# Slot logits of a soft mixture-of-experts layer: computed twice in two layouts, or once, stored and transposed

## The reference, cut to what matters

```
logits = (einsum('tzd,ed->tze', x, phi_w) + phi_b).reshape(t, z, n, p)
D = softmax(logits, axis=3)          # over the 32 slots of an expert
C = softmax(logits, axis=2)          # over the 64 experts of a slot
X_tilde = einsum('tznp,tzd->npd', D, x)      # summed over all 8 entries
X_tilde = tanh(normalise(clip(X_tilde)))
Y_tilde = einsum('npd,ndH->npH', X_tilde, expert_w) + expert_b
Y = einsum('tznp,npH->tzH', C, Y_tilde)
```

## Time and profile before

| what | value |
|---|---|
| median of 3 runs | 1195.12 us (1194.73 to 1200.56) |
| the profiled execution's own time | 1194.49 us |
| its span, first to last instruction | 1192.6 us |
| busy: PE, PEld, DVE, ACT, POOL | 1032.1, 765.7, 765.5, 518.0, 158.1 us |
| mean granted clock of PE | 0.948 |
| HBM read, written | 33.16 MB, 1.06 MB |
| mean DMA rate | 29 GB/s |

### The profile page before, as it was taken

One profiled execution on the slowest core, in us unless ns is written; L12 is line 12 of the kernel. 1 busy time (PEld: TensorE's weight loads), 2 busy tenths in 40 slices (PEclk: granted clock), 3 DMA queues, 4 the chain that ended last, 5 costly groups with the idle time before them and its releaser, 6 DMA issues.

```text
span 1192.6 us, 18208 instructions
## 1 busy us (share of the span) xinstructions
PE 1032.1 (87%) x6734; PEld 765.7 (64%) x6760; DVE 765.5 (64%) x1829; ACT 518.0 (43%) x836; POOL 158.1 (13%) x166
## 2 busy tenths in 40 slices
PE   3989999998648899999999953788999999998755
PEld 2878888886436667776766733566666666666432
DVE  4565555554574678888888777536567676676432
ACT  1245445435322554465557312235455536543510
POOL 1120110100307300000000004201212022011000
PEclk9999999999768999999999987999999999999976
DMA  8010000000300221001300003000000000000000
GB/s 319 2 28 15 14 15 14 14 14 2 124 0 1 85 93 54 17 38 53 124 1 1 1 1 107 1 1 1 1 6 1 6 1 5 6 1 6 5 5 5
DMA packets 11800, 35.39 MB, mean 30 GB/s; under 512 B 2570, under 2 KB 5818, under 8 KB 10944
## 3 DMA queue, kind: packets, MB, share of 16 engines
q1 hardware_dynamic: 10464, 33.14, 7.8%
q10 hardware_dynamic: 1152, 1.05, 0.3%
q0 software_dynamic: 96, 0.04, 0.0%
HBM read 33.16 MB, written 1.06 MB: 29 GB/s over the span
## 4 chain that ended last, share of the span: by engine, by line
PE 58%; issue 18%; DVE 15%; DVEq 4%; ACT 2%; POOL 1%; POOLq 1%; another core or an unknown queue 0%; ACTq 0%
PE ps L1118 5%; PE ps L1104 5%; PE ps L836 5%; PE ps L1001 3%; PE ps L1046 3%; PE ps L1258 3%; PE ps L1179 3%; PE ps L1159 2%; DVE arena L1822 2%; PE ps L1197 2%; PE ps L870 2%; PE ps L1021 2%; PE ps L846 2%; PE ps L882 2%; PE ps L994 2%
## 5 line engine op out<-in xcount | busy, mean ns | idle before, releaser
L1926 DVE TENSOR_REDUCE arena<-ps 128x8 f32<-128x2048 f32 x32 | 73.3, 2291 | 37.3 <-PE ps L1159 37.3
L1465 ACT ACTIVATE arena<-ps 128x2048 f32<-128x2048 f32 x32 | 60.1, 1879 | 57.5 <-PE ps L1183 57.5
L1104 PE MATMUL ps<-uR,arena 128*128 128x256 f32 x256 | 74.6, 386 | 0.1
L1258 PE MATMUL ps<-arena 128*128 128x512 f32 x128 | 68.2, 657 | 5.5 <-DVE xacc L2000 4.4
L1021 PE MATMUL ps<-arena,uR 128*128 128x512 f32 x128 | 67.7, 610 | 3.5 <-ACT arena L1411 3.0
L1046 PE MATMUL ps<-arena 128*128 128x128 f32 x512 | 64.9, 281 | 6.7 <-DVE arena L1838 5.0
L1046 PEld LDWEIGHTS ps<-arena 128*128 128x128 f32 x512 | 62.4, 196 | 12.1 <-issue 7.9
L1118 PE MATMUL ps<-arena 128*128 128x256 f32 x256 | 63.9, 395 | 6.6 <-DVE arena L1907 3.7
L1438 ACT ACTIVATE arena<-ps 128x512 f32<-128x512 f32 x64 | 38.0, 598 | 60.5 <-PE ps L1105 54.1
L1118 PEld LDWEIGHTS ps<-arena 128*128 128x128 f32 x256 | 47.9, 194 | 20.0 <-issue 9.6
L836 PE MATMUL ps<-arena 128*128 128x256 f32 x256 | 58.0, 384 | 0.0
(11 more groups left out here) (381 smaller groups left out, 2355.5 us busy)
## 6 DMA issues: line engine op xcount, KB each, us to landing
arena<-in_skills SPq DMA_DIRECT2D x16, 768.0 KB, 5.7
arena<-in_expert_w SPq DMA_DIRECT2D x2, 2048.0 KB, 8.3
arena<-in_l_experts SPq DMA_DIRECT2D x8, 386.5 KB, 3.1
arena<-in_consts_b SPq DMA_DIRECT2D x1, 1152.0 KB, 9.5
x2R<-in_x ACTq DMA_DIRECT2D x8, 128.0 KB, 6.5
arena<-in_L_w SPq DMA_DIRECT2D x2, 512.0 KB, 12.1
arena<-in_phiC SPq DMA_DIRECT2D x1, 1024.0 KB, 12.6
arena<-in_expert_b SPq DMA_DIRECT2D x1, 1024.0 KB, 4.9
```

Source lines behind the costliest of these rows:

```text
L1104: mm(o, phiC[:, st_ * P:(st_ + 1) * P], uR[:, b, :], start=True, stop=False)
L1258: last = mm(low[:, 3, :], pm[:, 2 + j, k * P:(k + 1) * P], w2e[:, j, c * 512:(c + 1) * 512], start=j == 0, stop=j == 1)
L1465: av(pexp[:, t, gp].rearrange("p c h t -> p (c h t)"), scores[:, :, :].rearrange("p c t -> p (c t)"), ACT.Exp, scale=SCALE3).then_inc(s.sc ...
L1926: V.tensor_reduce(nm[:, k, :, 2 * gp:2 * gp + 2], scores[:, :, :].rearrange("p c (h t) -> p c h t", h=2), X, ALU.max, negate=True).then_in ...
```

## The change

The logits are made once, in LG. ACT's new step LC copies each tile out of PSUM into `raw` (four buffers of 1024 words, in the place of the no longer needed `hid`), DVE's LG takes both maxima there for 1024 slots at once, POOL's new step DS adds the negated maximum over slots and writes `eD`, and ACT's SH takes the exponential in SBUF. SP's new step KP stores each `raw` in a DRAM scratch. MT, SH and MC of PE and the copies of MT and MC of ACT are gone. LG of PE has three PSUM banks in place of two.

For the softmax over experts SP's new step BACK reads the logits of an entry back, tokens in partitions; POOL's CM adds the negated maximum over experts, ACT's CE takes the exponential, POOL's CA adds the halves, DVE's CB sums the rest, REC inverts, PE's CR transposes the reciprocals and DVE's RC copies them; PE's TC transposes the exponentials, and DVE's CN multiplies out of PSUM into `eC`, of which there is now one. CL, CSA, CSB and CSUM are gone. EWA and EWB load later, since `expert_w` goes where `hid` and `raw` lie. The constants `samep`, `selD`, `selP` go, and with them POOL's PX and some memsets. All of ORDER_BD is new. One wait for ACT's own pipe (a drain) is put ahead of SQ2. The core of the diff, by engine:

```diff
     # SP
-    LOAD.0 LOAD.1 LOAD.2 EWA.0 LOAD.3 LOAD.4 LOAD.5 LOAD.6 EWB.0 LOAD.7 EBD.0 ST.0 ST.1 ST.2 ST.3 ST.4 ST.5 ST.6
+    KP0.3 KP1.3 KP2.3 KP3.3 LOAD.6 KP0.4 KP1.4 KP2.4 KP3.4 LOAD.7 KP0.5 KP1.5 KP2.5 KP3.5 EWA.0 KP0.6 KP1.6 KP2.6
+    KP3.6 BACK.0 KP0.7 KP1.7 KP2.7 KP3.7 EWB.0 BACK.1 EBD.0 BACK.2 BACK.3 BACK.4 BACK.5 ST.0 BACK.6 ST.1 BACK.7 ST.2
...
+                for j in range(4):
+                    if n == f"KP{j}":
+                        sp.wait_ge(s.raw_copied, at(b, 8, 2 * j + 1))
+                        sp.dma_start(raw_d[b, j // 2, j % 2], raw[j]).then_inc(kept[j], 16)
+                if n == "EWB":
+                    sp.wait_ge(s.max_ready, 8 * NB)
+                    sp.wait_ge(s.shifted, 4 * NB)
+                    for j in range(4):
+                        sp.wait_ge(kept[j], 16 * NB)
...
+                if n == "BACK":
+                    if b == 0:
+                        sp.wait_ge(s.uC_mm, NB)
...
+                    for k in range(K):
+                        sp.dma_start(cT[u][k].rearrange("p (h c) -> p h c", h=2),
+                                     raw_d[b, :, k].rearrange("h p c -> p h c")).then_inc(raw_back[u], 16)
     # PE
-                        mm(high[:, c, :], uR[:, b, k * P:(k + 1) * P], phiC[:, col:col + 512], start=True, stop=False)
-                        mm(high[:, c, :], ones_rows, phib3[:, col:col + 512], start=False, stop=True).then_inc(s.lg_mm, 1)
+                        bank = high[:, LG_BANK[i % 3], :]
+                        mm(bank, uR[:, b, k * P:(k + 1) * P], phiC[:, col:col + 512], start=True, stop=False)
+                        mm(bank, ones_rows, phib3[:, col:col + 512], start=False, stop=True).then_inc(s.lg_mm, 1)
...
-                        mm(o, phiC[:, st_ * P:(st_ + 1) * P], uR[:, b, :], start=True, stop=False)
-                        last = mm(o, selPx[:, st_, :], mcR[:, b, :], start=False, stop=True)
+                        for k in range(K):
+                            st_ = 2 * a + t
+                            last = tr(low[:, a % 2, t * T + k * P:t * T + (k + 1) * P], cT[u][k][:, st_ * P:(st_ + 1) * P], ident)
     # ACT
+                    if n == f"LC{st_}":
+                        act.wait_ge(s.lg_mm, at(b, 8, st_))
...
+                        av(raw[j][:, c * 512:(c + 1) * 512], high[:, LG_BANK[i % 3], :], ACT.Copy).then_inc(s.raw_copied, 1)
+                    if n == f"SH{j}":
+                        act.wait_ge(s.shifted, at(b, 4, j))
+                        av(eD[j // 2][:, j % 2, :], eD[j // 2][:, j % 2, :], ACT.Exp).then_inc(s.eD_ready, 1)
+                    if n == f"CE{k}":
+                        act.wait_ge(s.c_shifted, at(b, 2, k))
+                        av(cT[u][k], cT[u][k], ACT.Exp).then_inc(s.c_exp, 1)
     # DVE
+                        lg = raw[j].rearrange("p (n q) -> p n q", q=PSLOT)
+                        V.tensor_reduce(nmd[j % 2], lg, X, ALU.max, negate=True).then_inc(s.max_ready, 1)
+                        V.tensor_reduce(nmc[:, k, h, :], lg.rearrange("p n q -> p q n"), X, ALU.max,
+                                        negate=True).then_inc(s.max_ready, 1)
+                        V.reduce_sum(csum[:, k * PSLOT:(k + 1) * PSLOT], halved[k].rearrange("p (n q) -> p q n", q=PSLOT),
+                                     X).then_inc(s.csum_ready, 1)
-                    some = eC[u][:, 4 * q:4 * q + 4, :]
-                    V.tensor_tensor(some, some, rC.unsqueeze(1).to_broadcast([P, 4, T]), ALU.mult).then_inc(s.C_ready, 1)
+                    V.tensor_tensor(eC[:, 2 * a:2 * a + 2, :], low[:, a % 2, :].rearrange("p (t c) -> p t c", t=2),
+                                    rC.unsqueeze(1).to_broadcast([P, 2, T]), ALU.mult).then_inc(s.eC_ready, 1)
     # POOL
-    W.0 WA.0 W.1 RSZ.0 WA.1 W.2 WA.2 W.3 RSZ.1 WA.3 W.4 WA.4 W.5 WA.5 RSZ.2 W.6 WA.6 W.7 WA.7 RSZ.3 RSZ.4 RSZ.5
+    W.0 W.1 WA.1 W.2 WA.2 W.3 WA.3 W.4 WA.4 W.5 WA.5 W.6 WA.6 W.7 WA.7 RSZ.0 RSZ.1 DS0.0 DS1.0 RSZ.2 DS2.0 RSZ.3 DS3.0
...
+    RSZ.7 DS0.5 DS1.5 DS2.5 DS3.5 DS0.6 DS1.6 DS2.6 DS3.6 CM0.0 CM1.0 DS0.7 DS1.7 CA0.0 DS2.7 CA1.0 DS3.7 CM0.1 CM1.1
+    JR0.0 VZ.0 JR1.0 CA0.1 CA1.1 CM0.2 CM1.2 CA0.2 QM.0 CA1.2 CM0.3 CM1.3 CA0.3 CA1.3 QM.1 CM0.4 CM1.4 RS1.0 CA0.4
...
+                        tile = [P, 32, PSLOT]
+                        G.tensor_tensor(eD[h][:, k, :].rearrange("p (n q) -> p n q", q=PSLOT),
+                                        raw[j].rearrange("p (n q) -> p n q", q=PSLOT),
+                                        nmd[j % 2].unsqueeze(2).to_broadcast(tile), ALU.add).then_inc(s.shifted, 1)
+                        G.tensor_tensor(c, c, mcA[:, b, k * PSLOT:(k + 1) * PSLOT].unsqueeze(1).to_broadcast([P, NSLOT, PSLOT]),
+                                        ALU.add).then_inc(s.c_shifted, 1)
+                        G.tensor_tensor(halved[k], cT[u][k][:, 0:HALF], cT[u][k][:, HALF:2 * HALF], ALU.add).then_inc(s.c_halved, 1)
```

More of the change, by code:

```diff
@@ L162 @@
[L162 to L166, removed]
@@ L249 @@
[L249 to L253 removed]
+    BC0.0 BC1.0 Z.0 ZT.0 BC0.1 SG0.0 SU0.0 SG1.0 SU1.0 SG2.0 SU2.0 SG3.0 SU3.0 SG4.0 SU4.0 SG5.0 SU5.0 BC1.1 UC.0 Z.1
@@ new lines @@
+    DS0.1 DS1.1 DS2.1 DS3.1 RSZ.4 DS0.2 DS1.2 DS2.2 DS3.2 DS0.3 RSZ.5 DS1.3 DS2.3 DS3.3 DS0.4 RSZ.6 DS1.4 DS2.4 DS3.4
+    RSZ.7 DS0.5 DS1.5 DS2.5 DS3.5 DS0.6 DS1.6 DS2.6 DS3.6 CM0.0 CM1.0 DS0.7 DS1.7 CA0.0 DS2.7 CA1.0 DS3.7 CM0.1 CM1.1
+    JR0.0 VZ.0 JR1.0 CA0.1 CA1.1 CM0.2 CM1.2 CA0.2 QM.0 CA1.2 CM0.3 CM1.3 CA0.3 CA1.3 QM.1 CM0.4 CM1.4 RS1.0 CA0.4
+    CA1.4 QM.2 CM0.5 CM1.5 CA0.5 CA1.5 RS1.1 RS2.0 QM.3 CM0.6 CM1.6 CA0.6 CA1.6 RS1.2 QM.4 RS2.1 CM0.7 CM1.7 CA0.7
+    RS1.3 CA1.7 QM.5 RS2.2 RS1.4 RS2.3 QM.6 RS1.5 QM.7 RS2.4 RS1.6 RS2.5 RS1.7 RS2.6 RS2.7""",
@@ L608, in build @@
         pexp = flat.rearrange("p (k a b h t) -> p k a b h t", k=K, a=2, b=4, h=2)
-        eC = [te([P, ST, T]) for _ in range(2)]
+        eC = te([P, ST, T])
+        cT0 = te([P, K, 2 * HALF])
         xn = te([P, ST, P])
@@ L1105, in step_d @@
-                        last = mm(o, selPx[:, st_, :], mcR[:, b, :], start=False, stop=True)
-                    last.then_inc(s.cl_mm, 1)
-                if n == "CSUM":
-                    pe.wait_ge(s.csum_ready, at(b))
-                    if b == 0:
-                        pe.wait_ge(s.b_loaded, all_b)
-                    mm(low[:, 0, 0:T], con("samep"), csumS[:, :], start=True, stop=True).then_inc(s.csum_mm, 1)
+                        for k in range(K):
+                            st_ = 2 * a + t
+                            last = tr(low[:, a % 2, t * T + k * P:t * T + (k + 1) * P], cT[u][k][:, st_ * P:(st_ + 1) * P], ident)
@@ L1117, in step_d @@
                     for t in range(4 * q, 4 * q + 4):
-                        last = mm(low[:, 1, 0:T], ytl[:, t, :], eC[u][:, t, :], start=t == 0, stop=t == ST - 1)
+                        last = mm(low[:, 1, 0:T], ytl[:, t, :], eC[:, t, :], start=t == 0, stop=t == ST - 1)
                     if q == 3:
@@ L1492, in step_d @@
                 if n == "SQ2":
+                    act.drain()
                     act.wait_ge(s.y3_ready, at(b))
```

444 lines of the change are left out of this document (198 added, 246 removed).

## The result

The changed kernel takes 1229.83 us (median of 4 runs, 1228.26 to 1232.32) against 1197.05 for the kernel before on the same chip: ratio 1.0273, interval 1.0238 to 1.0308. It is **slower**, where the prediction said 1166. The profiled execution has a span of 1230.5 us, 37.9 more than before.

The account below looks back on a forecast made before the run. PE was taken to set the pace, with DVE close behind in B. The terms 7 - 13 + 2 - 25 = -29 on 1194.5 gave 1166 us; the forecast's own bounds were 1150 to 1190, the wider range 1135 to 1200.

Parts of the forecast that it names:

- The start, +7: Start of B: POOL's back-to-back sums and products hold five DVE operations, first BC 7 us later; bounds 0 and 10.
- B, -13: Steady B: PE drops 2.3 us a batch, about 0.4 given back to POOL holding DVE; 1.9 x 7 = 13 us earlier.
- Tail and join, +2: From UC.7's end to Y0.0: BACK, CM, DS, CA and EWB queues take 81 us against 79, 2 us later.
- D, -25: Steady D: TC cheaper than CL saves PE 5.4 us a batch, a third given back; 3.6 x 7 = 25 us earlier.
- I let a third of POOL's time reach DVE: Steady D: POOL's 16 us a batch adds 5 to DVE's 35, giving 40, under PE's 42.
- a third of the 5.4: Steady D: the part of PE's 5.4 us saving a batch given back because PE will wait at times, leaving 3.6.
- PE stays fed: Rival: POOL and DVE seldom meet; B gives 29, D 38, start costs nothing, join 2: 1130 us; chance 0.2.
- GpSimd holds VectorE: Rival: every DS, CM, CA and QM stops DVE for its whole length, in B and D: 1245 us; chance 0.14.
- Late reads: Rival: 2 MB reads take 15 us, JR0.0 slips, join costs 17 instead of 2: 1181 us; chance 0.1.
- TC no cheaper: Rival: TC costs as much as CL because its four weight loads show; D gives nothing: 1190 us; chance 0.06.

Follow-up runs that it names:

- the five other runs with this start: The changed kernel with short CM, short reads, neighbouring words, only D's steps, or fourteen moves: 1183.05, 1194.65, 1214.85, 1168.92, 1191.28 us.
- the run with the old products' order: The changed kernel with only the first 23 steps of POOL's list reordered, RSZ.0 again behind two products W: 1229.34 us.
- the new lists: The changed kernel, same steps, with the order in PE, ACT, DVE and POOL lists of B and D laid out from its own trace: 1122.66 us.
- fitting lists: The changed kernel with lists laid out from measured durations, once (1122.66 us) and once more from the durations of that run (1113.21 us).
- shorter reads: The changed kernel with its own lists, BACK of entries 2 to 7 reading 128 of each 1024 words: 1194.65 us.
- below 1184: The kernel before with lists found in the same way from its own trace, as long a search: 1184.16 us.
- the short CM: CM on 64 words in place of 2048: 1183.05 us with the changed kernel's own lists; with new lists and neighbouring-word reduces as well, 1102.05 us.
- the lists at 1123 and 1113 us: The changed kernel with lists laid out from its own trace (1122.66 us), then once more from the durations of that run (1113.21 us).

## Why the prediction was wrong, point by point

**The start, +7.** The first BC came 7.7 us later (4.4 to 6.7 in the five other runs with this start), and the run with the old products' order shows the reason to be the one given. The size was in part luck: the prediction had five operations of DVE held, three near 331 us and two near 351. In the trace seven took 1.98 to 2.41 us between 324 and 340 us, where two did before, and none near 351. The step from there to the end was wrong: only 1.7 us were left at UC.0.

**B, -13; it was +19.6.** The work was about right: UC.0 to UC.7 takes 254.4 us with the new lists, 16.2 less than before, at 36.3 us a batch where the prediction looked for 37. With the change's own lists a batch took 41.5, and PE idled 38.0 us in the seven together. Here the prediction took PE's and DVE's work for the time of a batch, allowed 0.4 us for POOL, and nothing for waits at the heads of the lists.

**Tail and join, +2; it was -0.2.** This is the one place where the prediction followed the queues step by step, and the only stage that came out close. DS0.7 started 16.5 us behind the end of UC.7 (forecast 18), DS3.7 ended 33.7 behind it (35), and JR0 started at 742.60, 58.3 behind it (61). But the last link was another, so the 0.2 is partly luck: the prediction had DVE done first and JR0 waiting for POOL's own queue. The timelines:

```profile
731.20 8.33 POOL L2105 TENSOR_TENSOR arena<-arena,mcA 128x2048 f32<-128x2048 f32 x2 [13.17 <-DMA arena<-raw_scratch]
742.60 0.25 POOL L2073 TENSOR_SCALAR arena<-arena 128x8 f32<-128x8 f32 x1 [3.07 <-DVE arena L1849]
...
735.95 4.12 DVE L1843 TENSOR_SCALAR xacc<-xacc 128x1024 f32<-128x1024 f32 x1
```

POOL was through with CM1.1 at 739.53 and then waited 3.07 us for DVE's JC0, whose clip (L1843) took 4.12 us beside CM1.1; the same operation of JC1 took 0.69.

**D, -25; it was +4.8, and 12.0 more in the tail, which the prediction costed at nothing.** This is **the step that failed** most: "I let a third of POOL's time reach DVE ... I give back a third of the 5.4". It treats the waiting as a share of an engine's load. The waits are set by which step stands at the head of each list: with the change's own lists Y came every 47.6 us, past the 47 that the prediction had named as proof against itself (before it was 46.9 from start to start; the 47.4 took 7 us for the last Y step, which ran from 1070.0 to 1080.4), and with other lists every 40.6, under the 43 to 44 that it forecast. With the new lists the D tail falls to 126.5 us (122.6 before).

**What was left out.** "All of ORDER_BD is new" stood in the change, and no term stood for it in the sum. Nor did one for the clock: the prediction took prices at full speed, and PE, which idled more, ran part of D at its lower level: 19.6 us more busy time from Y.0 to Y.7 than with the new lists.

**The rivals.** *PE stays fed* (1130) was in total about what the work allows, 1113 to 1123 with fitting lists, though not by stages: B gave 16 and not 29, and the join 7.5 where it had 2 lost. *GpSimd holds VectorE* (1245) had the sign and nearly the time, for a reason that the runs reject: with all of POOL's work kept, other lists took 107 us off and shorter reads 35. From Y.0 to Y.7 the DVE operations that took over 0.1 us more than the median of their line add up to 9.3 us of excess, 1.3 a batch, where this rival needed 12.4. *Late reads* had the mechanism but put it in the join, where POOL waited 13.17 us for BACK.1 and JR0 still waited for DVE; it was in D, where each read waits for a buffer that TC7 frees. *TC no cheaper* is out: 0.53 us a step, and from Y.0 to Y.7 PE is busy 264.7 us with the new lists, where it was 312.5 before.

**The price of CM.** The Trainium skill, GPSIMD Engine Reference, section 3.1 Elementwise, gives 4.5 us for two inputs of 2048 words; CM took 3.81 (median), with one operand repeated. The measurement decides, and by it CM was shorter than either figure used.

**What stays open.** For which durations the change's lists were made, the runs don't show. Whether a second search would take the kernel before below 1184 wasn't tried. Of the 11 us that the short CM gives with the new lists, the part of the held copies (below) and that of the chain were not told apart.

## What to carry to other kernels

When a change moves work to other engines in a program whose lists are written out, follow each new step to the step that stands behind it in the same list, and ask when each is needed; load per engine says only what a fitting order could reach. Put a step that ends a long chain just ahead of its first user, not where it is first allowed. Lay a new order out with durations measured on the new kernel, as the lists at 1123 and 1113 us were, and judge a change only with an order that fits it.

## What the runs showed of the hardware that was not expected

A plain copy on DVE, with one operand in SBUF, was held by POOL too, which the prediction assumed only of operations with two. REC's copy of 256 words (group), and one instance with POOL's CM of that moment (timelines):

```profile
L1879 DVE COPY nC<-arena x8: 294/295/4235, 734.1 to 1027.8; 128x256 f32<-128x256 f32 x8
...
802.70 4.24 DVE L1879 COPY nC<-arena 128x256 f32<-128x256 f32 x1
...
802.28 8.32 POOL L2105 TENSOR_TENSOR arena<-arena,mcA 128x2048 f32<-128x2048 f32 x2 [18.69 <-DMA arena<-raw_scratch]
```

The copy takes 0.29 us alone and took 4.24 when CM had started 0.42 us ahead of it. The Trainium skill, SBUF — State Buffer, section SBUF: two separate sides, counts a VectorE operation in one of its fast modes, such as a float32 copy within SBUF, among those that exclude GpSimd; this row agrees. JC0's clip (4.12 us for 0.69, above) and a single-operand operation of the routing (L1747: 2.27 us, and 0.30 in the run with the old products' order) were held in the same way. In B such holds are rare: DVE's multiply of `eD` (L1822), with two operands in SBUF, has a median of 1.226 and a longest of 1.749 us over 32 instances, with POOL's DS busy in the same stage.

The other surprise was the size of the clock's part: of the 48.5 us between two orders of the same D, 19.6 were PE's own records at a lower granted clock.
